# Rows gathered in float32 with their shift and scale, eight gather buffers, expert numbers read ahead, and the last tile but one routed inside the aggregation

## The reference

```python
h = x @ W.T                      # gcn_conv, called twice
msg = h[src] * norm[:, None]
out = jax.ops.segment_sum(msg, dst, num_segments=n_nodes)
...
logits = xt @ router_w.T         # xt = layernorm of the sum, 3125 x 768, 8 experts
top_w, top_i = lax.top_k(jax.nn.softmax(logits, axis=-1), 2)
e_sel = jnp.max(top_i, axis=-1)  # one expert for each row
y = jax.nn.silu(xt @ W1e) @ W2e  # 768 -> 128 -> 768, kept where e_sel == e
x = x + y
```

## Time and profile before

| | us |
|---|---|
| median of 3 runs (2415.44 to 2418.89) | 2416.7 |
| time of the profiled execution | 2420.72 |
| its span | 2419.0 |
| aggregation: last matmul ends | 2265.2 |
| table ready | 2285.7 |
| first turn of the routed stage | 2293.97 |
| last turn, last scatter issued | 2401.26, 2412.0 |

### The profile page before, as it was taken

The page is one execution under the profiler, slowest core; times in us unless marked ns, Lnnn a source line. Parts: engine busy times, 40 slices in busy tenths (PEclk is TensorE's granted clock), DMA queues, the critical chain, the costliest instruction groups (busy, mean ns, idle before and its releaser), DMA issues.

```text
span 2419.0 us, 44796 instructions
## 1 busy us (share of the span) xinstructions
PE 2325.1 (96%) x16783; PEld 1585.8 (66%) x16783; DVE 1254.3 (52%) x2843; ACT 861.1 (36%) x1323; POOL 866.5 (36%) x615
## 2 busy tenths in 40 slices
PE   5999999999999999999999999999999999999597
PEld 3878787878666666676666666666665666666365
DVE  6757575745767676765214334434431544444444
ACT  3546464635747464552112222222220101111143
POOL 1001216567678787876631111111100000000266
PEclk9999999999999999999999999999999999999799
DMA  7888786653331313225237866777745655554287
GB/s 286 283 280 293 259 277 164 172 138 74 66 66 1 66 0 65 29 26 123 33 55 246 239 214 203 229 219 202 220 168 199 181 186 205 182 183 168 66 172 136
DMA packets 172421, 385.63 MB, mean 159 GB/s; under 512 B 74800, under 2 KB 81818, under 8 KB 166396
## 3 DMA queue, kind: packets, MB, share of 16 engines
q1 hardware_dynamic: 90220, 313.83, 37.7%
q0 software_dynamic: 71264, 40.45, 15.2%
q10 hardware_dynamic: 10800, 29.50, 3.3%
HBM read 222.76 MB, written 166.44 MB: 161 GB/s over the span
## 4 chain that ended last, share of the span: by engine, by line
PE 80%; DVE 7%; ACT 6%; issue 4%; DMA 2%; SPq 1%; POOL 0%; DVEq 0%; ACTq 0%; POOLq 0%
PE pair L1905 33%; PE pair L393 32%; PE pair L1721 5%; PE pair L1701 3%; PE pair L1651 2%; DVE arena L1355 2%; DVE arena L1361 2%; DVE arena L1357 2%; ACT arena L956 2%; PE pair L1710 1%; ACT arena L882 1%; DMA arena<-hl_dram,arena 1%; PE pair L1825 1%; PE pair L2042 1%; ACT arena L966 1%
## 5 line engine op out<-in xcount | busy, mean ns | idle before, releaser
L393 PE MATMUL pair<-arena 128*128 128x384 f16 (+3 forms) x5760 | 892.1, 316 | 5.3 <-issue 3.4
L747 POOL DMA_INDIRECT cells<-arena x392 | 656.1, 1674 | 559.1 <-DMA cells<-arena 413.1
L1905 PE MATMUL pair<-arena 128*128 128x384 f16 x4900 | 813.0, 326 | 0.9 <-DVE arena L1522 0.9
L393 PEld LDWEIGHTS pair<-arena 128*128 128x128 f16 x5760 | 563.7, 98 | 316.5 <-issue 6.6
L1905 PEld LDWEIGHTS pair<-arena 128*128 128x128 f16 x4900 | 473.6, 98 | 306.1 <-issue 1.2
L779 POOL DMA_INDIRECT slots<-arena x25 | 28.7, 1150 | 477.2 <-DVEq L1577 444.6
L1721 PE MATMUL pair<-arena 128*128 128x66 f32 x1200 | 155.7, 273 | 1.6 <-ACT arena L925 1.2
L925 ACT ACTIVATE arena<-pair,arena 128x256 f32<-128x256 f32 x300 | 125.8, 478 | 68.2 <-PE pair L1701 66.4
L1721 PEld LDWEIGHTS pair<-arena 128*128 128x128 f32 x1200 | 146.8, 193 | 4.3 <-ACT arena L925 1.5
L1029 ACT ACTIVATE arena<-arena 128x768 f32<-128x768 f32 x25 | 23.4, 935 | 333.8 <-DVE arena L1456 333.8
L765 POOL DMA_DIRECT2D arena<-cells x25 | 30.3, 1213 | 285.3 <-DMA arena<-cells 278.7
(11 more groups left out here) (202 smaller groups left out, 2447.7 us busy)
## 6 DMA issues: line engine op xcount, KB each, us to landing
cells<-arena SPq DMA_DIRECT2D x50, 800.0 KB
ahl_dram<-arena SPq DMA_DIRECT2D x23, 1600.0 KB, 11.0
arena<-ahl_dram SPq DMA_DIRECT2D x23, 1600.0 KB, 7.5
arena<-in_x SPq DMA_DIRECT2D x70, 384.0 KB
arena<-key_dram SPq DMA_DIRECT2D x28, 896.0 KB
arena<-cells SPq DMA_DIRECT2D x25, 800.0 KB, 7.6
arena<-cells POOLq DMA_DIRECT2D x25, 800.0 KB
split_w<-arena SPq DMA_DIRECT2D x32, 384.0 KB
```

The lines of the kernel that those rows point to most:

```text
L393: ins = nc.tensor.matmul(dst[half], left(k, a), right(k, b, half), start=start and n == 0, stop=stop and n == 2)
L747: nc.gpsimd.indirect_dma_start(cells[k], bass.IndirectOffsetOnAxis(ap=idx_all[:, m:m + 1], axis=0), val_all[:, m:m + 1], None, bounds_chec ...
L1905: ins = nc.tensor.matmul(pair[u][:, half, 0:HD], a[:, 0, s * P:(s + 1) * P], X[part][:, s, half * HD:(half + 1) * HD], start=(s == 0 and p ...
```

## The change

What it does:

- The stored row is no longer the normalised value in two fp16 halves. `z_rows` holds 770 float32 numbers for each node: the sum, `shift` = -mean x r and the scale r. The store of `z_out` to `out` goes; `fhl`, `low` and ACT's cast go with it. POOL's last scatter writes the finished row to `out` without an add, and DVE's `result` adds the gathered sum to PE's product.
- Turning is done in float32 (`turn32`, 6 transposes, into the two banks of a pair). ACT evicts the rounded high part, and DVE subtracts it from the same PSUM tile for the low part; DVE now waits for ACT. This holds for routing and for the routed stage. There ACT first computes the normalised tile `gx` from the gathered row (`rows_normal`).
- Eight gather buffers (NG) for six. A buffer is free when `result` has read it (`f_out`), no longer at the turn. `down` uses one PSUM pair for all tiles and waits for the `result` before; `up` uses banks 4 and 5; two pairs hold turned tiles.
- PE reads 16 expert numbers before its first turn instead of 3, and none after a tile until number 16.
- Tile T-2 is routed inside the aggregation of tile T-1, at steps 14, 18 and 23.
- The table is built for one entry on each partition (`row_no`), so its operations have 1 to 64 columns for up to 256, and four of them are made before the aggregation. POOL clears its gather buffers before the last `slots` scatter.

The diff, cut to its core:

```diff
-NG, NO = 6, 4
+NG, NO = 8, 4
+ZW = D + 2
+READ_FIRST = 16
...
-        hl_dram = dram("hl_dram", [NP, 2 * D], F16)
+        z_rows = dram("z_rows", [NP, ZW])
...
+        turned = lambda i: pair[i][:, :, :].rearrange("p a b -> p (a b)")[:, 0:D]
...
@@ POOL
             for n in range(T):
+                if n == T - 1:
+                    pool.wait_ge(g2_full, T)
+                    for u in range(NG):
+                        made.link(nc.gpsimd.memset(g_in[u], 0.0))
                 pool.wait_ge(f_slot, n + 1)
...
             def gather_rows(j):
                 pool.wait_ge(rows_ld[j % 4], 16 + 16 * (j // 4 + 1))
                 if j >= NG:
-                    pool.wait_ge(g_tr, j - NG + 1)
+                    pool.wait_ge(f_out, j - NG + 1)
...
-                    bounds_check=NP - 1, oob_is_err=False, compute_op=ALU.add).then_inc(added[j % NO], 16)
+                    bounds_check=NP - 1, oob_is_err=False).then_inc(added[j % NO], 16)
@@ ACT
-                nc.scalar.copy(rT[0], bank16(4)[:, 0:D]).then_inc(ev_hi, 1)
+                nc.scalar.copy(rT[0], turned(2)).then_inc(ev_hi, 1)
...
-                act.wait_ge(out_ev, n + 1)
-                act.dma_start(out[bass.ds(tile_at(n) * P, P), :], z_out[u]).then_inc(out_st[u], 16)
...
-                nc.scalar.copy(fhl[u][:, 0:D], fn).then_inc(hi_ready, 1)
-                act.wait_ge(lo_ready, T + n + 1)
-                act.dma_start(hl_dram[bass.ds(tile_at(n) * P, P), :], fhl[u]).then_inc(xn_st[u], 16)
+                act.dma_start(z_rows[bass.ds(tile_at(n) * P, P), :], z_out[u]).then_inc(out_st[u], 16)
...
+            def rows_normal(j):
+                q = j % NG
+                act.wait_ge(gathered[q], gathered_base[q] + 16 * (j // NG) + 16)
+                if j >= 2:
+                    act.wait_ge(g_tr, j - 1)
+                nc.scalar.activation(gx[j % 2], g_in[q][:, 0:D], ACT.Identity, bias=g_in[q][:, D:D + 1],
+                                     scale=g_in[q][:, D + 1:D + 2]).then_inc(f_norm, 1)
@@ DVE
+                cn.link(nc.vector.scalar_tensor_tensor(shift, lnb[:, u, 4:5], -1.0, r, ALU.mult, ALU.mult))
...
             def route_evict(n):
-                dve.wait_ge(tr_done, n + 1)
-                nc.vector.tensor_copy(rT[1], bank16(5)[:, 0:D]).then_inc(ev_lo, 1)
+                dve.wait_ge(ev_hi, T + n + 1)
+                nc.vector.tensor_tensor(rT[1], turned(2), rT[0], ALU.subtract).then_inc(ev_lo, 1)
...
             def rows_evict(j):
-                dve.wait_ge(g_tr, j + 1)
-                nc.vector.tensor_copy(fT[1][j % 2], bank16(1)[:, 0:D]).then_inc(fT_lo, 1)
+                dve.wait_ge(fT_hi, j + 1)
+                nc.vector.tensor_tensor(fT[1][j % 2], turned(j % 2), fT[0][j % 2], ALU.subtract).then_inc(fT_lo, 1)
...
-                nc.vector.tensor_copy(halves(fo[j % NO]), wide(2 + j % 2)).then_inc(f_out, 1)
+                nc.vector.tensor_tensor(halves(fo[j % NO]), wide(3), halves(g_in[j % NG][:, 0:D]), ALU.add)\
+                    .then_inc(f_out, 1)
@@ PE
+            def turn32(i, rows):
+                for k in range(K):
+                    ins = nc.tensor.transpose(turned(i)[:, k * P:(k + 1) * P], rows[:, k * P:(k + 1) * P], ident32)
+                return ins
...
+                    if isinstance(n, int) and n == T - 1:
+                        if s == 14:
+                            route_turn(n - 1, 1 - u)
+                        if s == 18:
+                            route_logits(n - 1)
+                        if s == 23:
+                            route_prefix(n - 1)
...
             def rows_turn(j):
-                q = j % NG
-                pe.wait_ge(gathered[q], gathered_base[q] + 16 * (j // NG) + 16)
-                if j:
-                    pe.wait_ge(fT_hi, j)
-                    pe.wait_ge(fT_lo, j)
-                turn(bank16(0), bank16(1), g_in[q][:, 0:D], g_in[q][:, D:2 * D]).then_inc(g_tr, 1)
+                pe.wait_ge(f_norm, f_norm_base + j + 1)
+                if j >= 2:
+                    pe.wait_ge(fT_lo, j - 1)
+                turn32(j % 2, gx[j % 2]).then_inc(g_tr, 1)
...
-                if not isinstance(j, int) or j >= 2:
-                    pe.wait_ge(f_out, j - 1)
+                if j:
+                    pe.wait_ge(f_out, j)
...
-            for j in range(3):
+            for j in range(READ_FIRST):
                 read_expert(j)
...
-                if j + 1 < FT:
+                if READ_FIRST <= j + 1 < FT:
                     read_expert(j + 1)
```

More of the change, by code:

```diff
@@ L253, in build @@
         lnb = at(RT + 19104, 2, 16)
-        g_in = [at(RX + D * u, 2 * D, dt=F16) for u in range(NG)]
-        g_in32 = [at(RX + D * u, D) for u in range(NG)]
-        FR = RX + NG * D
+        g_in = [at(RX + ZW * u, ZW) for u in range(NG)]
+        FR = RX + NG * ZW
         fT = [[at(FR + HD * (2 * part + u), D, dt=F16) for u in range(2)] for part in range(2)]
@@ L262, in build @@
         fo = [at(FR + 2048 + D * u, D) for u in range(NO)]
-        reach, reach_n = at(FR + 2048 + NO * D, FT, NX), at(FR + 2304 + NO * D, FT, NX)
+        ident32 = at(WST, P)
+        gx = [at(FR + 2560 + NO * D + D * u, D) for u in range(2)]
         TAB = WST + 2304
@@ L479, in build @@
         table = sem("table")
[L480 to L483 removed]
+        gathered, g_tr = [sem(f"gathered{u}") for u in range(6)] + strip_added, sem("g_tr")
+        gathered_base = [0] * 6 + [16 * ((T + 1 - u) // 2) for u in range(2)]
+        fT_hi, fT_lo, f_h, f_act, f_ahi = [sem(f"f_{n}") for n in ("T_hi", "T_lo", "h", "act", "ahi")]
+        f_alo, f_alo_base, f_y, f_y_base = k_cast, UNITS, kp_full, UNITS * TC
+        f_out, added = sem("f_out"), [sem("added0"), sem("added1"), far_st, scattered[0]]
         added_base = [0] * 2 + [16, 16 * G * groups[0]]
@@ L782, in _ @@
                     bounds_check=SLOTS - 1, oob_is_err=False).then_inc(slot_st, 16)
-            pool.wait_ge(g2_full, T)
-            for u in range(NG):
-                made.link(nc.gpsimd.memset(g_in32[u], 0.0))
             for u, stores in ((0, 13), (1, 12)):
-                pool.wait_ge(xn_st[u], 32 * stores)
                 pool.wait_ge(out_st[u], 16 * stores)
@@ L1119, in _ @@
             for j in range(FT):
+                if j + 3 < FT:
+                    rows_normal(j + 3)
                 if j + 2 < FT:
@@ L1586, in layer2 @@
                     choose(n - 1)
-                normal(n, u)
+                normal(n, u, i)
                 if late:
                     place(n - 1)
-                low(n, u)
-            over_tiles(dve, layer2)
+            over_tiles(dve, layer2, T - 2)
+            layer2(T - 2, 1, T // 2 - 1)
+            route_evict(T - 2)
+            choose(T - 2)
+            place(T - 2)
+            finish(T - 1, 0, T // 2)
+            statistics2(T - 1, 0)
+            normal(T - 1, 0, T // 2)
             route_evict(T - 1)
@@ L1616, in _ @@
-            ct.link(nc.vector.tensor_scalar(expert_i, expert_f, float(NX - 1), None, ALU.min))
+            ct.link(nc.vector.scalar_tensor_tensor(out=reach, in0=ends, scalar=row_no[:, 0:1], in1=ones8, op0=ALU.is_le,
+                                                   op1=ALU.mult, accum_out=expert_f[:, 0:1]))
+            ct.link(nc.vector.scalar_tensor_tensor(out=reach_n, in0=reach, scalar=1.0, in1=ntile, op0=ALU.mult,
+                                                   op1=ALU.mult, accum_out=first_f[:, 0:1]))
@@ L2011, in _ @@
             layer2(2, 0, 1)
-            with pe.Fori(0, (T - 3) // 2) as i:
+            with pe.Fori(0, (T - 5) // 2) as i:
                 layer2(2 * i + 3, 1, i + 1)
                 layer2(2 * i + 4, 0, i + 2)
-            for n in (T - 2, T - 1):
-                route_turn(n, n % 2)
-                route_logits(n)
-                route_prefix(n)
+            layer2(T - 2, 1, T // 2 - 1)
+            layer2(T - 1, 0, T // 2)
+            route_turn(T - 1, 0)
+            route_logits(T - 1)
+            route_prefix(T - 1)
             pe.wait_ge(f_slot, T)
-            nc.tensor.matmul(bank(4)[:, HD + 24:HD + 24 + NX], ones16, seen, start=True, stop=True,
+            nc.tensor.matmul(bank(5)[:, FREE + 24:FREE + 24 + NX], ones16, seen, start=True, stop=True,
                              skip_group_check=True).then_inc(f_prefix, 1)
```

114 lines of the change are left out of this document (56 added, 58 removed).

## The result

| | before | changed |
|---|---|---|
| median, same chip, 7 runs each | 2418.89 | 2427.16 us |
| range | 2415.44 to 2420.06 | 2422.25 to 2431.31 |
| profiled execution, its span | 2420.72, 2419.0 | 2423.93, 2422.2 |
| pace of the routed stage, first turn to last | 3.461 | 3.713 us |

The ratio of changed to before is 1.0033, 95% interval 1.0022 to 1.0044: slower by 8 us, where 2410 and a gain of 6.8 were forecast. This is not the whole result. No execution of one group comes near the other: 2422 to 2431 us in the first session, 2400 to 2405 us on chip D. Both results are real, and the experiments tell what lies between them.

The account below looks back on a forecast made before the run. PE was taken to bound the aggregation, then a serial chain, then the gather-buffer ring the routed tiles. Terms 2.5 + 1.1 - 2.8 - 8.1 + 0.5 = -6.8 us off the median 2416.7 gave 2410 us, range 2388 to 2424.

Parts of the forecast that it names:

- A: Aggregation: six float32 transposes hold PE 0.78 us a turn for 0.67, over 23 turns +2.5 us; bounds -7.6 and +20.5.
- Both rivals on this price: Float32 turn costs 0.34 us (whole kernel 2389 us, chance 0.15) or 1.56 us (2454 us, chance 0.17).
- B: Tile T-2 routed inside the aggregation: its turn, logits and prefix move the aggregation's end out, +1.1 us.
- C: Chain from last aggregation matmul to first routed turn: 26.1 us for 28.9, -2.8 us.
- D: Routed stage: with eight buffers, 3.20 us a tile for 3.46 over 31 intervals, -8.1 us; bounds 3.10 and 3.40.
- The cover of 0.6 us: Routed stage: turn and up fill 1.9 us, result ends 1.3 us after down, so `down` waits only 0.1 us a tile.
- E: End: last `down` waits for result 30, +1.4 us; last scatter no longer queues, 1.0 us less; together +0.5 us.
- the three rivals: Whole kernel: cheap transposes 2389 us (0.15), dear ones 2454 us (0.17), plain scatter as costly as adding 2416 us (0.13).
- dear turns: Slower rival: each float32 transpose runs as two records, 1.56 us a turn, +37 us, 2454 us; chance 0.17.
- small waits: Routed stage: `down` would wait briefly for the result before it, put at 0.1 us a tile.

Follow-up runs that it names:

- chip D: Chip of later sessions; the changed kernel, unaltered, took 2403.96 and 2401.63 us there, beside 2413.76 and 2413.14 of the kernel before.
- late_route: Changed kernel with a 128-column zero write behind each gather and tile T-2 routed after the aggregation again; ratio to the kernel before 0.9991.
- after_third: Changed kernel, unaltered, run a third time, on chip D; ratio to the kernel before 0.9950, pace 3.01 us.
- after_again: Changed kernel, unaltered, run a second time, as control on chip D; ratio to the kernel before 0.9962, pace 3.00 us.
- after_fixed: Changed kernel with expert 0's weights at fixed addresses for every routed tile; ratio to the kernel before 0.9976, pace 3.27 us.
- before_plain: Kernel before with its adding result scatter made a plain write; ratio to the kernel before 1.0025, pace 3.65 us.
- after_add: Changed kernel with the adding scatter of the kernel before; ratio to the kernel before 0.9965, pace 3.16 us.
- down2: Changed kernel with `down` in two PSUM pairs by turns and the turned tile in one; ratio to the kernel before 1.0012, pace 3.73 us.

## Why the prediction was wrong

**A, the turn in the aggregation: mechanism right, size off.** 0.66 us, not 0.78; 23 turns of it are -0.2 us, and without the moved tile the aggregation took 390.4 us for 390.8 before: the term is -0.4 for +2.5. A float32 transpose is one record, 0.11 us, not one of the two 0.13 us records of a product. Both rivals on this price are refuted, 0.34 and 1.56 us a turn. The Trainium skill, page "TensorE: Matmul & The Clock Gate", section "Terms", has the transpose mode four times faster for float32; a quarter of the 0.26 us product would be 0.065 us, an estimate. The trace does not show that: 0.11 us, some 0.4 of the product, with the weight load (0.14 us recorded each) beside it. The serial eviction was hidden, as said.

**B, tile T-2 moved in: right.** Forecast +1.1; 391.4 - 390.4 = +1.0 us.

**C, the chain: right in kind, 26.95 us for 26.1 (the forecast counted from 0.2 us earlier).** The count came 12.3 us after the aggregation (12.0 forecast), the table 2.6 us behind the count (2.7). What was missed is the `slots` scatter's way: the first row numbers could be loaded at 2280.10, 18.9 us after the end, where I had the landing at 17.2. The 16 reads ended before the first turn, which waits for ScalarE alone. The term is -1.8 for -2.8, and `late_route` shows that most of it, and more, hangs on the moved tile.

**D, the pace: the step that failed.** Forecast 3.20 us with bounds 3.10 and 3.40; it was 3.71 on the result's chip and 3.01 on chip D, both outside. The inventory of bounds was right in its parts: GpSimd's scatter 1.03 us, gathers no longer waited for, DMA share 0.55 to 0.64 (some 60% forecast). Two things were wrong. First, PE's own floor. The forecast said that 15 fewer reads of an expert number between the tiles gain nothing. Where signals are on time they gain 0.36 us each. In `after_third` the 12 intervals from turn to turn without a read are 2.63 to 2.97 us, mean 2.78 (as in the chain above), and the 16 from the first such read on (2333.0 us) are 2.98 to 3.26, mean 3.14; `after_again` has the same two means. The place in the stage is not the cause: `after_fixed`, which reads nothing and works out no address, has intervals of 2.63 us up to the last tile. One interval with a read, in the chain of `after_third`:

```profile
2355.82 0.85 PE pair L1680 x6
2356.66 1.09 PE pair L2077 x18
2357.75 0.05 issue
2357.80 1.15 PE pair L2090 x6
2358.95 0.01 issue
2358.97 0.84 PE pair L1680 x6
```

The turns of before that gave the 3.155 us all had a read between them, so 3.10 was no lower bound for the tiles without one. (The forecast also took the old turn off with its recorded 0.83 us, where part A has it hold PE 0.67: 3.155 - 0.67 + 0.66 = 3.15, which is what the tiles with a read took.) Second, and this turned the sign: the small wait of `down` for the result before it, put at 0.1 us a tile, was 13.7 us in 21 tiles, 0.65 each, nearly all of PE's 14.8 us of idle time between 2300 and 2380. The result itself waited for a late signal in the stretch shown, and the silu stood 18.2 us in waits that no record explains. The cover of 0.6 us was computed as if every engine learned of a product when it ended.

The clue was on record. The silu's line of before said 21.1 us idle, 6.0 of them "remote". I read what ended most of a wait and passed over the rest. A wait without a releaser on a one-core program is a question, and a change that removes slack (one pair for two, a second serial operation) may well multiply whatever the answer is.

**E, the end: +1.2 us for +0.5.** `down` of the last tile waited 1.26 us for result 30 (1.4 forecast), and from the last turn to the end of the last scatter it took 10.96 us for 10.8 before. From there to the end of the span it was 7.9 us for 7.0, which I had not counted. It goes with the plain scatter: `before_plain` has 8.0 us there, `after_add` 6.9.

**The sum.** With the measured terms on the result's chip: -0.4 + 1.0 - 1.8 + 7.8 + 1.2 = +7.8 us. The spans are only 3.2 us apart, because earlier, unchanged stages happened to take 4.6 us less in the second (the first `finish` at 1869.5 for 1874.1); 3.2 + 4.6 is the same 7.8, and the medians are 8.3 apart. On chip D the whole is -9.8 and -11.5 us for the -6.8 forecast: the sign came out as forecast, but at a pace below the forecast's lower bound, so its nearness is in part luck. None of the three rivals names what happened: the slower one was to come from dear turns, and it came at the place where I had forecast "small waits".

## What to carry to other kernels

Run the unchanged candidate beside every variant on the same chip before a cause is named: my pauses "worked" on chips that had nothing to cure. Give each idle time without a releaser its share in the sum before slack is taken away; `down2` hints that a second PSUM pair pays where signals are late. A price read from intervals that all hold the same small operation does not tell what they cost without it: compare intervals with and without. And a cheaper operation off the critical path can cost time, as the plain scatter did in `before_plain`, where signals were late.

## What the runs showed of the hardware

- TensorE's signals can reach the other engines long after the product's recorded end, by up to 3.6 us in the changed kernel and 4.0 in `before_plain`, several in a bunch, 0.07 us apart. This was seen in six kernels in the first two sessions and in none of 14 profiles on three other chips later, always in the routed stage with GpSimd's indirect transfers and never in the second aggregation (94 signals in the changed kernel, none late).
- A load of one expert number into a register of PE's sequencer between two tiles costs 0.36 us a tile where nothing else waits (3.14 us for 2.78, `after_third`). Before the first turn 16 of them took 0.66 us each, hidden.
- A float32 transpose of 128 x 128 costs TensorE 0.11 us, so six hold it as long as twelve fp16 ones (0.66 and 0.67 us).
- A plain scatter of 3072-byte rows costs GpSimd 1.03 us, an adding one 1.59 to 1.60. The DMA share of the stage was 0.96 with the adding scatter (`after_add`) and 0.64 with the plain one (`after_third`), and still the paces were only 3.16 and 3.01 us.
- A write of 128 columns on GpSimd takes 0.22 us, but waiting for it before the next scatter leaves 1.05 us between gather and scatter.
